# Regrouping the feed-forward tiles of a graph layer as three, three, three and one, and building the expert tile table with its entries on partitions

## The chip, the cores and the metric

The kernel runs on one core of one Trainium2 chip. The metric is the device time of one execution in microseconds. TensorE (PE in the profile) multiplies matrices into PSUM banks, VectorE (DVE) and ScalarE (ACT) move and reshape what lies there, GpSimd (POOL) starts the transfers whose addresses are computed, and SyncE (SP) starts most other transfers.

## The reference

A layer over 1250 nodes of 512 features: a graph part (neighbour sums, then a feed-forward net 512 to 1024 to 512), an attention part, and behind their sum a top-2 mixture of 16 experts.

```
xn = layernorm(x)
x = x + gnn(xn) + attention(xn)
    gnn: rst = (1 + eps) * xn + segment_sum(xn[src], dst)
         relu(rst @ W1 + b1) @ W2 + b2 + xn
y = layernorm(x)
probs = softmax(y @ router_w.T + router_b);  p, i = top_k(probs, 2)
x = x + sum over the 2 chosen experts of p * (gelu(y @ w1e.T + b1e) @ w2e.T + b2e)
```

## The kernel before

The nodes lie in ten tiles of 128 rows (the last has 98). Everything runs in one program with an instruction stream for each engine, written out by hand; the order on an engine is the order of the code, and semaphores join the streams. The stages are: first layer norm; projections and edge counting; attention with the neighbour sums between its steps; the graph part's feed-forward net, with the routing to experts inside it; a loop over pairs of expert tiles; and the last gathers and sums.

The change is in the net and the routing. `FC_TILES` (line 34) divides the ten tiles into groups, before of 3, 3, 2 and 2. For each group TensorE first makes the hidden layer: eight blocks `m` of 128 hidden features, each of 12 matmuls (line 1391: four slices of 128 features by three terms, since each operand is split into a high and a low part). A matmul has 128x128 weights and as many moving columns as the group has rows. ScalarE evacuates each block twice (lines 739 and 740: the value, and its high part) and VectorE subtracts (line 1057: the low part). Four PSUM banks hold blocks, so block `m` waits for the evacuation of block `m - 4`. Then comes the second product, `mix(t)` (line 1334), for each tile: 24 matmuls of 512 columns. VectorE adds the result to the residual (line 1070), takes mean and deviation, and writes the normalised tile `x2n` (line 1077).

The routing of a group runs inside the next one. `turn_x2n(t)` (line 1343) turns the normalised tile on TensorE, ScalarE copies it (line 751), and `route(t)` (line 1352) multiplies it with the router's weights. `pick(f)` on VectorE (lines 986 to 1002) finds the two experts of each row in 14 small steps, `ranks(f)` on TensorE (line 1359) counts for each row how many rows go to the same expert ahead of it, `place(f)` (lines 1013 to 1019) makes of that the two slots of each row, `tally(f)` adds up what is taken, and `weigh(f)` (lines 1036 to 1043) makes the gates. GpSimd then scatters the rows of `x2n` to their slots in memory (`slots`), with two transfers for each tile (line 597). For the groups but the last this happens around blocks 1, 3, 4, 6 and 7 of the next group's hidden layer.

For the last group nothing is left to lie beside. Its tiles are routed in a tail: turn, route, pick, ranks, place, and then the tile table (lines 1084 to 1102), which tells for each of up to 40 expert tiles which expert it has (`te`), where its weights lie (`lies_at`) and where its rows begin (`tbase`). VectorE computes it with the same numbers on all 128 partitions, a comparison of 40 tile numbers with 16 experts being 128x640. `route_ready` tells of it. SyncE waits for `route_ready` and for all 20 scatters (line 423) and starts the first gathers of sorted rows (line 425); the experts' loop follows on all engines. As soon as the hidden layer of the last group is done, SyncE starts the weights of five experts, 1 MB each (line 402), and ScalarE those of two more behind the copy of tile 9 (line 755).

## Time and profile before

| | |
|---|---|
| median of 3 runs | 771.63 us (769.15 to 772.4) |
| the profiled execution | 767.46 us |
| its span in the trace | 765.3 us |
| TensorE busy in it | 683.8 us, 89% |
| share of TensorE in the chain that ended last | 74% |
| groups of three tiles, 482.1 to 520.8 | 38.7 us |
| group three (two tiles), 520.8 to 548.1 | 27.3 us |
| last group (two tiles), 548.1 to 574.8 | 26.7 us |
| tail, 574.8 to 594.6 | 19.8 us |

Times in the trace count from the start of the span, on this one execution. A timeline row gives the start, the time that the instruction was busy, the engine, the line and the operation; the spacing of instructions that overlap is read from their starts. What stands in square brackets is how long the engine was idle before and what ended that. A row of the table of stretches gives the stretch and its length, then the busy time and count of PE, PEld (weight loads), DVE, ACT and POOL, the granted TensorE clock as a share of 2.4 GHz, the busy share of the DMA engines, and what they moved in GB/s.

### The profile page before, as it was taken

What the parts mean: (1) busy time and instruction counts of PE and PEld (TensorE: products, weight loads), DVE (VectorE), ACT (ScalarE), POOL (GpSimd) and SP (SyncE); (2) the same over time, 40 slices, a digit from 0 to 9 for tenths busy, and PEclk for the clock granted to TensorE, in tenths of its full rate; (3) what the DMA queues carried; (4) which work ended last, traced back from release to release, by engine and by line L of the source; (5) the groups of instructions that cost most, each with busy time, mean ns of one, the idle gap of its engine ahead of it and who ended that gap; (6) DMA issues with size and microseconds to landing.
All of it is one profiled execution on the core that took longest, in us unless ns stands there. A gap on an engine that the chain in (4) does not pass through costs nothing.

```text
span 765.3 us, 12446 instructions
## 1 busy us (share of the span) xinstructions
PE 683.8 (89%) x3840; PEld 449.8 (59%) x3841; DVE 469.4 (61%) x923; ACT 232.2 (30%) x472; POOL 177.2 (23%) x271
## 2 busy tenths in 40 slices
PE   4877999999999999999999999999993599999935
PEld 2544545455555555555555898988872466776601
DVE  5637674479888898797855994354456133233337
ACT  2312211133233233233335342334332233343300
POOL 6056353103123240322101500030322110000064
PEclk9998899999999999999999999999996599999955
DMA  9600000072543707273474800020247795333367
GB/s 294 191 0 0 1 0 3 1 276 78 215 177 115 287 6 277 94 254 133 162 262 164 355 1 0 1 84 1 83 181 307 254 373 172 128 116 116 131 192 237
DMA packets 48902, 109.48 MB, mean 143 GB/s; under 512 B 6842, under 2 KB 6858, under 8 KB 46384
## 3 DMA queue, kind: packets, MB, share of 16 engines
q1 hardware_dynamic: 43616, 85.82, 31.2%
q0 software_dynamic: 4912, 20.60, 7.8%
q10 hardware_dynamic: 288, 2.10, 0.6%
q8 instruction: 31, 0.51, 0.3%
q14 instruction: 55, 0.45, 0.2%
HBM read 47.35 MB, written 61.16 MB: 142 GB/s over the span
## 4 chain that ended last, share of the span: by engine, by line
PE 74%; DVE 9%; issue 7%; DMA 4%; POOL 3%; ACT 2%; SPq 1%; POOLq 0%; DVEq 0%; ACTq 0%
PE bank L1296 11%; PE bank L1279 9%; PE bank L1447 7%; PE bank L1215 7%; PE bank L1460 6%; PE bank L1334 6%; PE bank L1247 6%; PE bank L1391 6%; PE bank L1258 5%; PE bank L1179 4%; PE bank L1319 4%; DVE arena L895 3%; DMA arena<-in_x 2%; PE bank L1418 2%; POOL arena L625 1%
## 5 line engine op out<-in xcount | busy, mean ns | idle before, releaser
L895 DVE TENSOR_TENSOR arena<-iota,arena 125x384 f16<-125x384 f16 (+2 forms) x318 | 186.6, 648 | 23.4 <-PE bank L1179 14.1
L699 ACT ACTIVATE arena<-bank 128x416 f32<-128x416 f32 (+1 forms) x120 | 62.3, 519 | 146.9 <-PE bank L1279 143.9
L1296 PE MATMUL bank<-arena 128*64 128x416 f32 (+1 forms) x480 | 97.2, 524 | 3.3 <-DVE arena L936 2.8
L936 DVE TENSOR_SCALAR arena<-bank 128x416 f32<-128x416 f32 (+1 forms) x120 | 67.4, 587 | 42.8 <-PE bank L1279 42.7
L523 POOL COPY arena<-arena 125x12 f32 (+1 forms) x80 | 35.6, 445 | 197.8 <-DVE arena L895 103.2
L1247 PE MATMUL bank<-arena 128*128 128x416 f32 (+1 forms) x192 | 77.8, 555 | 3.1 <-DMA arena<-in_wqkv 1.7
L1114 DVE COPY arena<-arena 128x1024 f32 x30 | 20.8, 694 | 75.7 <-issue 64.3
L1447 PEld LDWEIGHTS bank<-arena 128*128 128x128 f32 x448 | 53.4, 199 | 20.7 <-issue 20.7
L1447 PE MATMUL bank<-arena 128*128 128x128 f32 x448 | 55.7, 285 | 9.8 <-issue 9.8
L1179 PE MATMUL bank<-arena 125*128 125x160 f16 x471 | 52.0, 235 | 11.3 <-DVE arena L895 10.7
L1179 PEld LDWEIGHTS bank<-arena 125*128 125x128 f16 x471 | 32.3, 98 | 43.4 <-issue 26.7
L1247 PEld LDWEIGHTS bank<-arena 128*128 128x128 f32 x192 | 37.5, 204 | 31.7 <-issue 29.8
L597 POOL DMA_INDIRECT slots<-arena,slot x20 | 20.0, 999 | 139.6 <-DVEq L1020 134.8
L1296 PEld LDWEIGHTS bank<-arena 128*64 128x64 f32 x480 | 30.6, 135 | 36.5 <-issue 26.7
L1460 PE MATMUL bank<-arena 128*128 x112 | 50.4, 592 | 0.0
L1279 PE MATMUL bank<-q_hi,k_hi 64*128 64x416 f32 (+1 forms) x240 | 48.8, 401 | 0.4 <-ACT arena L681 0.4
L625 POOL DMA_INDIRECT arena<-slots,slot x20 | 20.6, 1032 | 111.4 <-POOLq L621 105.6
L1215 PE MATMUL bank<-xn_hi,a_t 128*128 128x512 f32 x100 | 45.6, 456 | 0.0
L1279 PEld LDWEIGHTS bank<-q_hi,k_hi 64*128 64x128 f32 x240 | 22.3, 181 | 39.2 <-issue 38.5
L1279 PE MATMUL bank<-q_lo,k_hi 64*128 64x416 f32 (+1 forms) x240 | 42.6, 349 | 0.0
L1279 PE MATMUL bank<-q_hi,k_lo 64*128 64x416 f32 (+1 forms) x240 | 42.5, 348 | 0.0
L777 ACT ACT_TABLE_LOAD x14 | 18.0, 1283 | 74.4 <-PE bank L1447 74.4
(227 smaller groups left out, 1193.4 us busy)
## 6 DMA issues: line engine op xcount, KB each, us to landing
slots<-arena SPq DMA_DIRECT2D x6, 5376.0 KB, 17.2
slots<-arena SPq DMA_DIRECT2D x2, 5120.0 KB, 15.7
arena<-in_ew POOLq DMA_DIRECT2D x9, 1024.0 KB, 6.8
arena<-slots SPq DMA_DIRECT2D x32, 256.0 KB, 2.8
slots<-arena SPq DMA_DIRECT2D x28, 256.0 KB, 2.0
arena<-in_ew SPq DMA_DIRECT2D x5, 1024.0 KB, 14.1
arena<-in_x SPq DMA_DIRECT2D x8, 512.0 KB, 7.5
arena<-in_gw SPq DMA_DIRECT2D x2, 2048.0 KB, 17.8
```

Source lines behind the costliest of these rows:

```text
L699: act.activation(probs[0:kt, s % NPB, 0, 0:n], bank[2 * (s % 2)][0:kt, 0:n], ACT.Relu).then_inc(p0_ready, 1)
L895: ins = dve.tensor_tensor(hot[:, :, c], iota16[0:CE, 0:width].unsqueeze(1).to_broadcast([CE, n, width]), window_cols[:, i % WBUF, of, k0:k ...
L936: dve.tensor_single_scalar(probs[0:kt, s % NPB, 1, 0:n], bank[2 * (s % 2) + 1][0:kt, 0:n], 0.0, op=ALU.max).then_inc(p1_ready, 1)
L1179: return pe.matmul(window_at(w), of[:, at_slot:at_slot + P], of[:, at_slot + P:at_slot + OHW], start=start, stop=stop, skip_group_check=True)
L1215: ins = pe.matmul(bank[NB][:, :], a_t[:, g % 2, t, :], x[t][:, :], start=(t == 0 and x is xn_hi), stop=(t == NT - 1 and x is xn_lo), skip_ ...
L1247: ins = pe.matmul(bank[g % 5][:, 0:n], w_qkv[:, part, k, c:c + P], xn_t[:, k, o:o + n], start=(k == 0), stop=(k == KD - 1))
L1279: ins = pe.matmul(bank[2 * (s % 2) + a][0:kt, 0:n], k[p][half, t * P:t * P + kt], q[p][half, o:o + n], start=(i == 0), stop=(i == len(term ...
L1296: ins = pe.matmul(bank[AV][DH * a:DH * a + DH, 0:n], v_sb[0:kt, t, h * DH:h * DH + DH], probs[0:kt, s % NPB, a, 0:n], start=(t == 0), stop ...
L1334: ins = pe.matmul(bank[4 + t % 2][0:r, :], h[:, m, c:c + r], w, start=(m == 0 and i == 0), stop=(m == KH - 1 and i == 2))
L1391: ins = pe.matmul(bank[g % 4][:, 0:n], w[k][:, m * P:(m + 1) * P], r[k][:, o:o + n], start=(k == 0 and i == 0), stop=(k == KD - 1 and i == 2))
L1447: ins = pe.matmul(bank[a][:, m * P:(m + 1) * P], w1_now[:, a, k * DFF + m * P:k * DFF + m * P + P], xg_t[:, a, k, :], start=(k == 0), stop ...
L1460: ins = pe.matmul(bank[6 + a][:, :], hg_t[:, a, k, :], arena[:, bass.ds(lies[a] + KD * DFF + k * D, D)], start=(k == 0), stop=(k == KF - 1))
```

## The change

The groups are now tiles 0 to 2, 3 to 5, 6 to 8, and tile 9 alone. In the short last group the turn of tile 8 and the route of tile 7 stand behind block 3 (for other groups: block 1), the route of tile 8 behind block 6, the pick of group three behind block 7 (the last), its ranks inside the second product of tile 9, behind five of its eight parts, and its gates (`weigh`) after the tile table. `x2n` lies at another address, since tile 8 is now normalised while the weights that lie at its old place are still in use. The tile table has one of its 40 entries on each partition: comparisons are 40x16, and the three results are columns, which TensorE turns into a row of 3 times 40, from which VectorE copies them to one partition.

```diff
-FC_TILES = [range(0, 3), range(3, 6), range(6, 8), range(8, 10)]
+FC_TILES = [range(0, 3), range(3, 6), range(6, 9), range(9, 10)]
...
-        x2n = at(XN, [NT, D])
+        x2n = at(VALB, [NT, D])
...
-        tef, tsum = at(5120, [MAXT]), at(5280, [MAXT])
+        tef, tsum = at(5120, [1], parts=MAXT), at(5280, [1], parts=MAXT)
+        cols = at(5360, [3], parts=MAXT)
...
+        table = sb("table", [1, 3, MAXT], i32)
+        te, lies_at, tbase = (table[:, c, :] for c in range(3))
...
-                    if tiles[0] and m == 5:
+                    if tiles[0] and m == (KH - 1 if f == len(FC_TILES) - 1 else 5):
                         exponents(f - 1)
...
-                    if f and m == 4:
+                    short = f == len(FC_TILES) - 1
+                    if f and m == (KH - 1 if short else 4):
                         pick(f - 1)
-                    if f and m == 7:
+                    if f and m == KH - 1:
                         place(f - 1)
                         tally(f - 1)
-                        weigh(f - 1)
+                        if not short:
+                            weigh(f - 1)
...
-            link(dve.tensor_tensor(tcmp, tidx[:, :].unsqueeze(2).to_broadcast([P, MAXT, EXP]),
-                                   tend.unsqueeze(1).to_broadcast([P, MAXT, EXP]), ALU.is_ge))
-            dve.tensor_reduce(tef, tcmp, X, ALU.add)
-            dve.tensor_copy(npair[:, :], red2[:, 0:1])
-            link(dve.tensor_tensor(tskip, tcmp, skip.unsqueeze(1).to_broadcast([P, MAXT, EXP]), ALU.mult))
-            dve.tensor_scalar(te[:, :], tef, float(EXP - 1), None, ALU.min)
...
+            link(dve.tensor_scalar(tcmp, tend[0:MAXT, :], tidx[:, :], None, ALU.is_le))
+            link(dve.tensor_reduce(tef, tcmp, X, ALU.add))
+            link(dve.tensor_tensor(tskip, tcmp, skip[0:MAXT, :], ALU.mult))
+            dve.tensor_scalar(cols[:, 0:1], tef, float(EXP - 1), None, ALU.min)
             link(dve.tensor_reduce(tsum, tskip, X, ALU.add))
...
+            dve.sem_inc(table_ready, 1)
+            link(dve.tensor_copy(npair[:, :], red2[0:1, 0:1]))
+            link(dve.tensor_single_scalar(npair[:, :], npair[:, :], 1, op=ALU.arith_shift_right))
+            dve.wait_ge(table_ps, 1)
+            link(dve.tensor_copy(table[:, :, :], bank[2][0:1, 0:3 * MAXT].rearrange("p (c n) -> p c n", c=3)))
             dve.sem_inc(route_ready, 1)
+            weigh(len(FC_TILES) - 2)
             weigh(len(FC_TILES) - 1)
...
                 for m in range(KH):
+                    if t == NT - 1 and m == 5:
+                        ranks(len(FC_TILES) - 2)
...
-                    if o and m == 1:
+                    short = f == len(FC_TILES) - 1
+                    if o and m == (3 if short else 1):
                         turn_x2n(tiles[0] - 1)
                         route(tiles[0] - 2)
-                    if o and m == 3:
+                    if o and m == (6 if short else 3):
                         route(tiles[0] - 1)
-                    if o and m == 6:
+                    if o and m == 6 and not short:
                         ranks(f - 1)
...
-            route(NT - 2)
             turn_x2n(NT - 1)
             route(NT - 1)
             ranks(len(FC_TILES) - 1)
+            pe.wait_ge(table_ready, 1)
+            for c in range(3):
+                ins = pe.transpose(bank[2][0:1, c * MAXT:(c + 1) * MAXT], cols[:, c:c + 1], ident[0:MAXT, 0:MAXT])
+            ins.then_inc(table_ps, 1)
```

How the change moves instructions, on TensorE at the start of the tail. Before, from the end of the second product of tile 9 (512 columns) on: a turn and a route for tile 8, then for tile 9, the ranks, and the turns of eight tiles' gates (16x128).

```order
L1334 MATMUL bank<-w_lo,h_hi 98x512
L1343 MATMUL bank<-ident,arena 128x128 x4
L1352 MATMUL bank<-rw_sb,arena 128x16 x4
L1343 MATMUL bank<-ident,arena 128x128 x4
L1352 MATMUL bank<-rw_sb,arena 128x16 x4
```

Now, in the changed kernel, with the last ranks and what follows them (its line numbers differ):

```order
L1340 MATMUL bank<-w_lo,h_hi 98x512
L1349 MATMUL bank<-ident,arena 128x128 x4
L1358 MATMUL bank<-rw_sb,arena 128x16 x4
L1365 MATMUL bank<-seen,ones 128x16
L1365 MATMUL bank<-mask,tri 128x16
L1365 MATMUL bank<-seen,ones 128x16
L1365 MATMUL bank<-mask,ones 128x16
L1423 MATMUL bank<-ident,arena 1x40 x3
L1436 MATMUL bank<-ident,arena 16x128 x9
```

One turn and one route leave the tail for the last hidden layer; three transposes of the table's columns come in, ahead of the turns of the gates, which are nine tiles' now.

The ranks of group three in the changed kernel, on TensorE inside the second product of tile 9 (before they stood between blocks 6 and 7 of the hidden layer):

```order
L1340 MATMUL bank<-w_lo,h_hi 98x512
L1365 MATMUL bank<-seen,ones 128x16
L1365 MATMUL bank<-mask,tri 128x16
L1365 MATMUL bank<-seen,ones 128x16
L1365 MATMUL bank<-mask,ones 128x16
L1365 MATMUL bank<-mask,tri 128x16
L1365 MATMUL bank<-seen,ones 128x16
L1365 MATMUL bank<-mask,ones 128x16 x2
L1365 MATMUL bank<-mask,tri 128x16
L1340 MATMUL bank<-w_hi,h_hi 98x512
```

Nine matmuls of 16 columns split that product after 15 of its 24.

The tile table on VectorE, before:

```order
L1093 TENSOR_TENSOR arena<-tidx,arena 128x640
L1095 TENSOR_REDUCE arena<-arena 128x40
L1096 CAST npair<-arena 128x1
L1097 TENSOR_TENSOR arena<-arena 128x640
L1098 TENSOR_SCALAR te<-arena 128x40
L1099 TENSOR_SCALAR npair<-npair 128x1
L1100 TENSOR_REDUCE arena<-arena 128x40
L1101 TENSOR_SCALAR lies_at<-te 128x40
L1102 SCALAR_TENSOR_TENSOR tbase<-tidx,arena 128x40
```

and now:

```order
L1095 TENSOR_SCALAR arena<-arena,tidx 40x16
L1096 TENSOR_REDUCE arena<-arena 40x1
L1097 TENSOR_TENSOR arena<-arena 40x16
L1098 TENSOR_SCALAR arena<-arena 40x1
L1099 TENSOR_REDUCE arena<-arena 40x1
L1100 TENSOR_SCALAR arena<-arena 40x1
L1101 SCALAR_TENSOR_TENSOR arena<-tidx,arena 40x1
L1104 CAST npair<-arena 1x1
L1105 TENSOR_SCALAR npair<-npair 1x1
L1107 CAST table<-bank 1x120
L1036 TENSOR_REDUCE arena<-arena 128x3
```

The wide steps are gone, a copy from PSUM ends the table, and the gates of group three (128x3) follow it.

## Rows read from the trace of the kernel before

**Rows 1.** The page: share of the span by engine in the chain that ended last.

```profile
PE 74%; DVE 9%; issue 7%; DMA 4%; POOL 3%; ACT 2%; SPq 1%; POOLq 0%; DVEq 0%; ACTq 0%
```

**Rows 2.** The tail in the table of stretches.

```profile
574.80:594.60 19.80, 6.74 (x40) 4.17 (x38) 12.89 (x51) 4.94 (x13) 4.38 (x4) 0.61 0.69 279
```

**Rows 3.** TensorE's timeline: starts of groups two, three, four, and a second product.

```profile
482.14 0.42 PE L1391 MATMUL bank<-rst_hi,w_hi 128*128 128x384 f32 x1
482.40 0.34 PE L1391 MATMUL bank<-rst_lo,w_hi 128*128 128x384 f32 x1
482.57 0.34 PE L1391 MATMUL bank<-rst_hi,w_lo 128*128 128x384 f32 x1
...
520.79 0.36 PE L1391 MATMUL bank<-rst_hi,w_hi 128*128 128x256 f32 x1
...
548.13 0.35 PE L1391 MATMUL bank<-rst_hi,w_hi 128*128 128x226 f32 x1
548.32 0.27 PE L1391 MATMUL bank<-rst_lo,w_hi 128*128 128x226 f32 x1
548.43 0.27 PE L1391 MATMUL bank<-rst_hi,w_lo 128*128 128x226 f32 x1
...
563.41 0.40 PE L1334 MATMUL bank<-w_hi,h_hi 128*128 128x512 f32 x1
```

**Rows 4.** TensorE's timeline: the routing passes ahead of 482.14.

```profile
481.33 0.96 PE L1352 MATMUL bank<-rw_sb,arena 128*128 128x16 f32 x8
```

**Rows 5.** A pick's first step, TensorE's waits for ranks, the last split (timelines).

```profile
496.70 0.20 DVE L986 TENSOR_TENSOR arena<-bank,rb_sb 128x48 f32<-128x48 f32 x1
...
500.02 0.18 PE L1359 MATMUL bank<-seen,ones 128*128 128x16 bf16 x1 [0.72 <-DVEq L1003]
...
561.85 0.18 PE L1359 MATMUL bank<-seen,ones 128*128 128x16 bf16 x1 [1.60 <-DVEq L1003]
...
564.43 0.40 DVE L1057 TENSOR_TENSOR h_lo<-arena,h_hi 128x226 fp32r<-128x226 f32 x1 [1.85 <-ACT h_hi L740]
```

**Rows 6.** Timelines of VectorE and TensorE in the tail.

```profile
574.77 0.69 DVE L1070 TENSOR_TENSOR arena<-arena,bank 98x512 f32<-98x512 f32 x1 [2.65 <-PE bank L1334]
...
579.11 1.89 PE L1352 MATMUL bank<-rw_sb,arena 128*128 128x16 f32 x8 [0.69 <-ACT arena L751]
...
585.77 0.16 DVE L1019 CAST slot<-arena 128x2 int32<-128x2 f32 x1
...
588.28 0.82 DVE L1093 TENSOR_TENSOR arena<-tidx,arena 128x640 f32<-128x640 f32 x1
...
591.88 0.19 DVE L1102 SCALAR_TENSOR_TENSOR tbase<-tidx,arena 128x40 int32<-128x40 f32 x1
```

**Rows 7.** Stretches again: the full DMA engines, and where the clock falls.

```profile
566.00:585.00 19.00, 13.37 (x72) 10.12 (x70) 9.36 (x37) 3.11 (x6) 3.85 (x4) 0.85 1.01 412
...
579.00:580.00 1.00, 0.89 (x5) 0.89 (x5) 0.00 (x0) 0.69 (x2) 0.00 (x0) 0.56 0.99 418
```

**Rows 8.** Timelines of ScalarE's, POOL's and SyncE's queues: transfers issued around the tail.

```profile
578.47 0.87 ACTq L755 DMA_DIRECT2D arena<-in_ew  x2
...
586.27 0.96 POOL L597 DMA_INDIRECT slots<-arena,slot  x1 [15.33 <-DVEq L1020]
...
590.24 1.33 POOL L597 DMA_INDIRECT slots<-arena,slot  x1 [0.30 <-issue]
...
594.62 1.47 SPq L425 DMA_DIRECT2D arena<-slots  x2
```

**Rows 9.** A like transposition and copy early in the kernel (timelines).

```profile
39.83 0.30 PE L1162 MATMUL bank<-ident,mincol 80*1 80x80 f32 x2
...
40.17 0.31 DVE L852 COPY minrow<-bank 1x160 f32<-1x160 f32 x1 [2.65 <-PE bank L1162]
```

**Rows 10.** Groups by shape, 440 to 606: busy us, then mean ns.

```profile
L725 ACT ACT_TABLE_LOAD x4 | 5.1, 1283 | 0.4 <-issue 0.3
L739 ACT ACTIVATE arena<-bank,b 128x226 f32<-128x226 f32 x8 | 3.6, 449 | 4.4 <-PE bank L1391 4.4
```

More of the change, by code:

```diff
@@ L227, in layer @@
         thr = sb("thr", [P, NT])
-        tidx = sb("tidx", [P, MAXT])
+        tidx = sb("tidx", [MAXT, 1])
         below = sb("below", [P, EXP, EXP])
@@ L290, in layer @@
         hid_ps, hid_hi, hid_lo = sem("hid_ps"), sem("hid_hi"), sem("hid_lo")
-        mix_ps, x2_ready = sem("mix_ps"), sem("x2_ready")
+        mix_ps, x2_ready, table_ready, table_ps = (sem(n) for n in ("mix_ps", "x2_ready", "table_ready", "table_ps"))
         var2_ready, std2_ready, x2n_ready, x2nt_ps, x2nt_saved, logit_ps = (
@@ L494, in _ @@
             ramp(thr[:, :], [[P, NT]])
-            ramp(tidx[:, :], [[1, MAXT]])
+            ramp(tidx[:, :], [[0, 1]], 0, 1)
             ramp(ebase[:, :], [[CAP, EXP]])
@@ L1092, in _ @@
             dve.tensor_scalar(red2[:, 0:1], tend[:, EXP - 1:EXP], 1.0, None, ALU.add)
-            link(dve.tensor_tensor(tcmp, tidx[:, :].unsqueeze(2).to_broadcast([P, MAXT, EXP]),
-                                   tend.unsqueeze(1).to_broadcast([P, MAXT, EXP]), ALU.is_ge))
-            dve.tensor_reduce(tef, tcmp, X, ALU.add)
-            dve.tensor_copy(npair[:, :], red2[:, 0:1])
-            link(dve.tensor_tensor(tskip, tcmp, skip.unsqueeze(1).to_broadcast([P, MAXT, EXP]), ALU.mult))
-            dve.tensor_scalar(te[:, :], tef, float(EXP - 1), None, ALU.min)
-            dve.tensor_single_scalar(npair[:, :], npair[:, :], 1, op=ALU.arith_shift_right)
+            link(dve.tensor_scalar(tcmp, tend[0:MAXT, :], tidx[:, :], None, ALU.is_le))
+            link(dve.tensor_reduce(tef, tcmp, X, ALU.add))
+            link(dve.tensor_tensor(tskip, tcmp, skip[0:MAXT, :], ALU.mult))
+            dve.tensor_scalar(cols[:, 0:1], tef, float(EXP - 1), None, ALU.min)
             link(dve.tensor_reduce(tsum, tskip, X, ALU.add))
-            dve.tensor_scalar(lies_at[:, :], te[:, :], float(-EW), float(expert_at(0)), ALU.mult, ALU.add)
-            link(dve.scalar_tensor_tensor(out=tbase[:, :], in0=tidx[:, :], scalar=float(P), in1=tsum,
+            dve.tensor_scalar(cols[:, 1:2], cols[:, 0:1], float(-EW), float(expert_at(0)), ALU.mult, ALU.add)
+            link(dve.scalar_tensor_tensor(out=cols[:, 2:3], in0=tidx[:, :], scalar=float(P), in1=tsum,
                                           op0=ALU.mult, op1=ALU.add))
+            dve.sem_inc(table_ready, 1)
[3 more added lines that the diff above has]
+            link(dve.tensor_copy(table[:, :, :], bank[2][0:1, 0:3 * MAXT].rearrange("p (c n) -> p c n", c=3)))
             dve.sem_inc(route_ready, 1)
+            weigh(len(FC_TILES) - 2)
             weigh(len(FC_TILES) - 1)
```

9 lines of the change are left out of this document (3 added, 6 removed).

## The prediction

> **What bounds the kernel now.** I read the page first: TensorE is busy 89% of a span of 765.3 us and carries 74% of the chain of waits [rows 1]. So columns and weight loads that are added to TensorE before the experts' loop cost time, unless they stand in an idle stretch. The table of stretches comes next [rows 2]: from 574.8 to 594.6 TensorE does 6.74 us of work in 19.8. TensorE's timeline [rows 3] cuts what lies ahead: group two (tiles 3 to 5) from 482.14, group three (tiles 6, 7) from 520.79, the last group (tiles 8, 9) from 548.13, its second product from 563.41. The reader is to see two regimes. Up to 574.8 TensorE is the bound, with an idle of one or two microseconds in each group. Then a serial chain is the bound: normalise tile 9, turn it, route, pick, rank, place, make the tile table, scatter, gather. The change moves work between the two, so I price it on one ruler, the time at which SyncE issues the first gather of sorted rows, 594.62 [rows 8]. From there on the program is the same (one row more or less of register work in TensorE's loop), so the shift of that moment is the shift of the end.
>
> **Group three, +11.3 us.** With three tiles it becomes what group two is now: same shapes, same turns, routes and ranks. Group two takes 482.14 to 520.79, 38.65 us, group three 520.79 to 548.13, 27.34 [rows 3]: +11.31. In that stands one tile's second product, some 5.6 us, that leaves the last group. The new last group starts at 548.13 + 11.31 = 559.44.
>
> **Hidden layer of the last group, -2.4 us.** Before: 548.13 to 563.41, 15.28 us [rows 3], with 96 matmuls of 226 columns. After: 96 of 98 columns, a shape that the trace doesn't show. Starts are 0.17 us apart at 384 columns (0.174 over a block) and 0.11 at 226 [rows 3], some 0.4 us per thousand columns over a fixed 0.015. By columns alone 98 would take 0.056. The nearest row speaks against that: the routing matmuls of 16 columns, whose stationary operand is also 128x128 in four bytes, run as eight passes from 481.33 to 482.14 [rows 3, 4], 0.10 each, so something that doesn't depend on the columns sets a floor. I take 0.105, nearer to the 16-column row; ends 0.056 and 0.12, a little over the 226-column rate. 96 x 0.105 = 10.1, one turn 0.44 (four transposes at the 0.11 of a mid-sized matmul), two routes of 0.81. Then a wait. The turn of tile 8 now stands behind the fourth block, 5 us into the group; add, norm, turn and copy take 4.3 us for tile 9 (574.77 to 579.11 [rows 6]) and start before the group does, so x2n is there. But ScalarE copies the turned tile first (0.6), and only then evacuates block 0, with two instructions (0.45 each at 226 columns [rows 10], so about 0.35 at 98, overlapping to 0.6), while TensorE needs block 0's bank for the fifth block. The route hides 0.8 of that; I put 0.75 us. Sum 12.9 against 15.3. The idle of 1.60 us for a pick [rows 5] is gone from here, since the ranks leave this stretch.
>
> The Trainium skill (TensorE: Matmul & The Clock Gate, "LDWEIGHTS") gives a load as P/1.2 ns with P the stationary columns, 107 ns for 128. By that the 96 matmuls are 10.3 us, and the trace agrees with it at 16 columns. Its formula for the gap of a matmul by itself, N/2.4 + 2.5 ns ("Back-to-back issue gap"), gives 43 ns for 98 columns: that is the first rival's price, and by it the sum would be some 6 us lower than mine.
>
> **Second product and ranks, -4.5 us.** Before: 563.41 to the residual add of tile 9 at 574.77 [rows 3, 6], 11.36 for two tiles, 5.68 each. After: one tile, with the ranks of group three put in after 15 of its 24 matmuls. Call the product's start M. The last block's split starts 1.02 after M now (564.43 [rows 5]) and its pick's first step a fraction later; narrower blocks save about that fraction. The pick of three tiles takes 3.32 (496.70 to 500.02 in group two [rows 5]), so the mask is there at M+4.35. TensorE comes at M+3.5, waits 0.9 and spends 0.25 on the ranks. The add starts at M + 5.7 + 1.15 = M+6.85. Place (1.2) and tally (0.7) of group three end at M+6.6, just before the add needs VectorE: slack 0.25, and what runs over goes onto the path one to one. The exponents of group three bring two table loads of 1.28 us [rows 10]; they end by M+4, ahead of the standard deviation of tile 9 at M+8.8. The change: 6.85 - 11.36 = -4.5.
>
> **Tail up to the slots, -0.25 us.** Add at 574.77, last slot cast at 585.77, slots posted about 586.0 [rows 6]: 11.2 us of instructions that cost their fixed time. A tile of 16 columns in place of 32 saves 0.01 to 0.02 on each of some twenty. The route of tile 9 takes 1.89 us, against 0.81 in group two [rows 4, 6], since the granted clock falls to 0.50 (1.2 GHz) in 579 to 580 [rows 7], five microseconds after dense work ended. I let that stand; at full clock it is -0.8.
>
> **Scatter and table, -2.7 us, given back in part.** POOL issues four scatters for tiles 8 and 9, from 586.27 to 590.24, and the gather follows 4.4 us behind the last [rows 8]. With two scatters the last goes out 2.7 us earlier relative to the slots, at +1.5 in place of +4.2, and the gather at slots +5.9 in place of +8.6. The table has to keep up. Now it is done at 592.1, 6.1 after the slots [rows 6]. A pass over 128x640 takes 0.82 [rows 6]; four of them and their small companions fill 3.85 us from 588.28 on. Seven steps on 40 partitions at 0.2 each, some of them side by side, are 1.3. New are three transposes and a copy: the like of them early in the kernel took 0.34 from matmul to copy and 0.31 for the copy [rows 9], and I add 0.2 for load and half clock and 0.1 for the post. The table is ready 4.7 after the slots, and the scatters land at 4.9: the scatters stay last, with a slack of 0.2. If the transposes take a microsecond longer, the path takes 0.8 of it.
>
> The six scatters of tiles 6 to 8 occupy POOL from M+6 to M+13.7 at 1.27 each; the last slots come at M+17.8. Free. The gates of group three are made after the table (1.6 us) and TensorE turns them before the gathered rows; done about M+25.8, while those rows are some three microseconds from an issue at M+24.5. Free too, with a slack of 1.7.
>
> What gives back is the DMA. Five experts' weights (1 MB each) are issued as the hidden layer ends, two more at 578.47 [rows 8], and the 16 engines are full from 566 to 585 at 412 GB/s [rows 7], to about M+22, just before the late scatters. Now the two loads come at M+10.5 and there are 1.57 MB of early scatters in place of 1.05, so the backlog ends at M+23.3. But tile 9's scatters go out at M+18.1 and M+19.3, inside it. Free of load they land at M+22.7; behind the whole backlog at about M+25.8. I take +0.8, for engines that share.
>
> The Trainium skill (DMA: Bandwidth & Descriptors, "Queues, rings and completion order") has each engine go round its queues packet by packet, so a scatter isn't held behind all that was issued earlier. That speaks for the small price; no row here shows how late a scatter lands under load.
>
> **The sum.** +11.3 - 2.4 - 4.5 - 0.25 - 2.7 + 0.8 = +2.25 us. Checked on the ruler: M = 559.44 + 12.9 = 572.3, gather at M + 22.7 + 0.8 + 1.0 = 596.8 against 594.6. The profiled execution took 767.46 us (its span and 2.2 around it), so 769.7 on its terms; the median of the three runs is 771.63, which makes 773.8. In words: a tail shortened by three microseconds is paid with four on TensorE and one in the DMA, because 384 + 98 columns don't cost what 256 + 226 do when a floor lies under the short matmuls. A measurement of this kernel can tell about 0.5%, 3.9 us, from no change.
>
> **Rivals.** *Columns alone set the short matmul.* At 0.056 the hidden blocks take 5.4 us, not 10.1, and the wait of 0.75 stays. M is 4.6 earlier, the sum -2.35, 769.3. For it: the line through two widths. Against: 0.10 at 16 columns. If the last route also runs at full clock and the DMA costs nothing, it is -4, faster by 0.5%.
>
> *The scatter waits for the weights.* Tile 9's scatter lands behind the backlog, at M+25.8: 3.1 in place of 0.8, sum +4.5, 776.1, slower by 0.6%. For it: the DMA engines have no slack up to 585 [rows 7], and there is more to move now. Against: the queues differ. It decides from a landing later than M+25.2.
>
> *The tail gains less than it moves.* Ranks late, place running over the add, or a table behind the landing: each up to 1 us, 775.
>
> *TensorE's idles pay for the regrouping.* The waits for ranks are 0.72 in group two and 1.60 in the last group [rows 5]. What of them falls away is in the sum already; a further gain of 1 us would have to come from group three, whose copy of group two is exact. 773.
>
> **How the numbers follow.** A shift of 0 to +3.8, with the last two rivals' common sizes: 0.58. Columns alone: 0.17, of which 0.08 beyond -0.5%. Scatter behind the weights: 0.15. Several small delays together, or a short matmul dearer than 0.12, beyond +0.5%: 0.05. Something that I don't see, gaining over 0.5%: 0.05. Faster 0.13, same 0.67, slower 0.20. The range takes in the first rival's centre and the second's: 768.5 to 777.5.
>
> **What would show it.** Right: group three's period 38.6 us; starts of the 98-column matmuls 0.10 to 0.11 apart; hidden layer of the last group near 13 us; a wait of about a microsecond before the ranks inside the last product; first gather 1.5 to 3 us later than 594.62; the loop unchanged. Wrong: starts 0.06 apart; a gather before 594; SyncE's wait ending on the table rather than on the scatters; other gaps in the loop.

## The result and the profile after

The changed kernel takes 782.23 us (median of 4 runs, 780.73 to 785.39), the kernel before 770.39 (4 runs, 766.84 to 772.4): a ratio of 1.016, interval 1.0129 to 1.0191. It is slower by 11.8 us. The forecast was 773.8, with a range up to 777.5. The profiled execution of the changed kernel is its longest, 785.39 us with a span of 783.4; that of before was among the shorter ones, so the two traces differ by more (18.1 us of span) than the medians do.

The chain by engine of the page looks much as before [rows 1]; no share has moved by more than two points:

```profile
PE 75%; DVE 7%; issue 6%; DMA 5%; POOL 4%; SPq 2%; ACT 1%; POOLq 0%; ACTq 0%; DVEq 0%
```

So the page's summary doesn't tell it; the timeline does. Of TensorE after (hidden layer L1397, second product L1340), answering to [rows 3]:

```profile
561.80 0.29 PE L1397 MATMUL bank<-rst_hi,w_hi 128*128 128x98 f32 x1
561.93 0.28 PE L1397 MATMUL bank<-rst_lo,w_hi 128*128 128x98 f32 x1
562.04 0.27 PE L1397 MATMUL bank<-rst_hi,w_lo 128*128 128x98 f32 x1
...
567.71 0.41 PE L1397 MATMUL bank<-rst_lo,w_hi 128*128 128x98 f32 x1
567.92 0.41 PE L1397 MATMUL bank<-rst_hi,w_lo 128*128 128x98 f32 x1
568.13 0.41 PE L1397 MATMUL bank<-rst_hi,w_hi 128*128 128x98 f32 x1
...
583.84 0.71 PE L1340 MATMUL bank<-w_hi,h_hi 128*98 128x512 f32 x1
584.34 0.63 PE L1340 MATMUL bank<-w_hi,h_lo 128*98 128x512 f32 x1
```

The reader is to see the starts: 0.11 apart for the first three microseconds, 0.21 apart six microseconds later, for the same instructions. The last hidden layer lasts from 561.80 to 583.84, 22.0 us, where two tiles took 15.3 before. The table of stretches says why (columns as in the section before the change):

```profile
563.00:564.00 1.00, 1.00 (x11) 1.00 (x10) 0.66 (x2) 0.00 (x0) 0.00 (x0) 1.00 0.00 0
564.00:565.00 1.00, 1.00 (x10) 1.00 (x9) 0.00 (x0) 0.00 (x0) 0.00 (x0) 0.86 0.00 0
565.00:566.00 1.00, 1.00 (x6) 1.00 (x6) 0.00 (x0) 0.00 (x0) 0.00 (x0) 0.50 0.00 0
566.00:575.00 9.00, 9.00 (x44) 9.00 (x44) 1.04 (x4) 2.78 (x11) 0.00 (x0) 0.50 0.01 2
...
584.00:588.00 4.00, 4.00 (x11) 2.73 (x11) 2.79 (x14) 3.38 (x5) 0.00 (x0) 0.50 0.70 244
588.00:589.00 1.00, 1.00 (x4) 0.64 (x4) 0.07 (x1) 0.00 (x0) 0.00 (x0) 0.70 0.98 410
```

TensorE's granted clock falls to its lower level, 1.2 GHz (0.50), at about 564.7, and is back at 2.4 at 588.6, some five microseconds after the 512-column matmuls began. In all that time the second column, TensorE's busy time, is the whole stretch: by the records the engine never stood idle. It is no accident of one execution: the mean granted clock over the whole span is 0.933 to 0.935 in all four runs, 0.950 in the profile of before.

The tail, answering to [rows 5] and [rows 6]: the ranks of group three inside the second product, the residual add, the last route, the last slot, the table's copy.

```profile
589.55 0.18 PE L1365 MATMUL bank<-seen,ones 128*128 128x16 bf16 x1
...
592.21 0.69 DVE L1072 TENSOR_TENSOR arena<-arena,bank 98x512 f32<-98x512 f32 x1 [0.28 <-PE bank L1340]
...
596.96 1.89 PE L1358 MATMUL bank<-rw_sb,arena 128*128 128x16 f32 x8 [0.69 <-issue]
...
603.21 0.14 DVE L1019 CAST slot<-arena 128x1 int32<-128x1 f32 x1
...
607.43 0.27 DVE L1107 CAST table<-bank 1x120 int32<-1x120 f32 x1
```

And the queues, answering to [rows 8]: GpSimd's last scatter, SyncE's first gather.

```profile
604.98 0.94 POOL L597 DMA_INDIRECT slots<-arena,slot  x1 [0.30 <-issue]
...
610.70 1.46 SPq L425 DMA_DIRECT2D arena<-slots  x2
```

The table of milestones below is made of such rows. All kernels are put on one ruler, the start of group two, since what lies ahead of it is the same code and still varies by some 3 us between executions (it starts at 482.14 before, 484.47 after). The last column is the span less the time of the first gather, that is the experts' loop and the last sums. All in us.

| kernel | last hidden layer | second product to last add | add to last slot | last slot to last scatter | scatter to first gather | group two to first gather | gather to end |
|---|---|---|---|---|---|---|---|
| before | 15.28 | 11.36 | 11.00 | 4.47 | 4.38 | 112.48 | 170.7 |
| after | 22.04 | 8.37 | 11.00 | 1.77 | 5.72 | 126.23 | 172.7 |
| pad226 | 13.55 | 6.96 | 11.12 | 1.77 | 6.62 | 117.35 | 171.2 |
| pad160 | 13.49 | 6.99 | 11.09 | 1.77 | 6.68 | 117.34 | 170.9 |
| wide | 18.03 | 6.96 | 10.10 | 1.77 | 6.72 | 120.89 | 171.2 |
| place226 | 14.97 | 5.79 | 10.34 | 1.78 | 8.72 | 118.92 | 170.6 |
| late226 | 13.55 | 6.97 | 10.50 | 1.78 | 4.16 | 114.28 | 183.2 |
| paced226 | 13.55 | 6.98 | 11.11 | 1.76 | 4.12 | 114.86 | 177.5 |
| place_paced | 14.98 | 5.79 | 9.99 | 1.78 | 4.47 | 114.32 | 173.8 |
| place_paced_warm | 14.96 | 5.81 | 9.76 | 1.77 | 4.40 | 114.02 | 180.5 |
| table_only | 16.23 | 11.99 | 11.47 | 4.29 | 3.99 | 113.97 | 171.1 |
| late_before | 16.30 | 11.95 | 11.46 | 4.46 | 4.37 | 114.53 | 184.4 |
| warm_before | 15.14 | 11.36 | 10.17 | 4.47 | 4.39 | 113.07 | 171.2 |
| warm2_before | 16.45 | 11.87 | 10.16 | 4.46 | 4.39 | 113.32 | 172.4 |

After less before, term by term: group three +11.3, last hidden layer +6.8, second product -3.0, scatters and what follows -2.7 and +1.3, together +13.7 at the first gather, and two more in the loop. That is more than the 11.8 of the medians. One reason is that the profile of before is a good draw: a short fall of the clock, told in the last section, is absent from it, and in table_only and late_before it goes with a gather 1.5 to 2 us later. SyncE's wait ends on the scatters in both kernels, not on the table.

### The profile page after: what moved, and what is told of

The parts are those of the page before. It is cut to its first block, busy times and chain, and to the rows that moved or that the text cites. A ratio compares the mean times of both kernels' runs of the same rounds, so it can differ in the third digit from the quotient of the medians.

```text
span 783.4 us, 12455 instructions
## 1 busy us (share of the span) xinstructions
PE 703.1 (90%) x3843; PEld 466.7 (60%) x3844; DVE 467.5 (60%) x924; ACT 232.2 (30%) x472; POOL 174.9 (22%) x271
## 4 chain that ended last, share of the span: by engine, by line
PE 75%; DVE 7%; issue 6%; DMA 5%; POOL 4%; SPq 2%; ACT 1%; POOLq 0%; ACTq 0%; DVEq 0%
PE bank L1301 11%; PE bank L1284 9%; PE bank L1397 7%; PE bank L1340 7%; PE bank L1457 7%; PE bank L1220 6%; PE bank L1252 6%; PE bank L1470 6%; PE bank L1263 4%; PE bank L1184 4%; PE bank L1324 4%; DVE arena L895 3%; POOL arena L625 2%; DMA arena<-in_x 2%; PE bank L1428 2%
## 5 line engine op out<-in xcount | busy, mean ns | idle before, releaser
L895 DVE TENSOR_TENSOR arena<-iota,arena 125x384 f16<-125x384 f16 (+2 forms) x318 | 186.6, 647 | 23.4 <-PE bank L1184 14.1
L1252 PE MATMUL bank<-arena 128*128 128x416 f32 (+1 forms) x192 | 79.5, 565 | 2.1 <-ACT arena L640 2.1
L1457 PE MATMUL bank<-arena 128*128 128x128 f32 x448 | 55.9, 285 | 10.3 <-issue 10.3
L1184 PEld LDWEIGHTS bank<-arena 125*128 125x128 f16 x471 | 32.5, 98 | 43.4 <-issue 26.8
L1397 PE MATMUL bank<-rst_hi,w_hi 128*128 128x384 f32 (+1 forms) x128 | 45.0, 351 | 0.0
L1397 PE MATMUL bank<-rst_hi,w_lo 128*128 128x384 f32 (+1 forms) x128 | 44.5, 348 | 0.0
L1397 PE MATMUL bank<-rst_lo,w_hi 128*128 128x384 f32 (+1 forms) x128 | 44.2, 345 | 0.0
```

What stands on the lines that cost most here:

```text
L895: ins = dve.tensor_tensor(hot[:, :, c], iota16[0:CE, 0:width].unsqueeze(1).to_broadcast([CE, n, width]), window_cols[:, i % WBUF, of, k0:k ...
L1184: return pe.matmul(window_at(w), of[:, at_slot:at_slot + P], of[:, at_slot + P:at_slot + OHW], start=start, stop=stop, skip_group_check=True)
L1252: ins = pe.matmul(bank[g % 5][:, 0:n], w_qkv[:, part, k, c:c + P], xn_t[:, k, o:o + n], start=(k == 0), stop=(k == KD - 1))
L1397: ins = pe.matmul(bank[g % 4][:, 0:n], w[k][:, m * P:(m + 1) * P], r[k][:, o:o + n], start=(k == 0 and i == 0), stop=(k == KD - 1 and i == 2))
L1457: ins = pe.matmul(bank[a][:, m * P:(m + 1) * P], w1_now[:, a, k * DFF + m * P:k * DFF + m * P + P], xg_t[:, a, k, :], start=(k == 0), stop ...
```

## The experiments

Theories. **A**: with 98 columns each matmul is so short against its weight load that the array itself is mostly idle, and the clock falls for that, although the records show the engine busy; a wider matmul of the same spacing would keep it. **B**: the width has nothing to do with it. **C**: short matmuls of any kind in that place take it down. **D**: the experts' weights, which fill the DMA engines as the last scatters go out, make them land late. **E**: the new place of the picks and ranks is what costs. (The recorded text of late226 calls the opposite of D its rival E; it is not this one.)

### Width alone: pad226 and pad160

Every matmul of the last hidden layer is given the 128 rows ahead of tile 9's 98 too (62 in pad160), and ScalarE reads the last 98 results; the others are thrown away. 96 weights, 96 instructions, the same values kept.

```diff
+                            e = max(226 - n, 0)
-                            ins = pe.matmul(bank[g % 4][:, 0:n], w[k][:, m * P:(m + 1) * P], r[k][:, o:o + n],
+                            ins = pe.matmul(bank[g % 4][:, 0:n + e], w[k][:, m * P:(m + 1) * P], r[k][:, o - e:o + n],
```

> The changed kernel, but the 96 hidden-layer matmuls of the last group stream 226 columns (rows of tile 8 again, thrown away) in place of 98; evacuations read the last 98. Theory A (the granted clock fell to 1.2 GHz because 98 columns leave the array idle under each weight load): spacing stays 0.111 us as for 98 columns at full clock, the clock stays 1.00 up to the tail, the last hidden layer takes 13.5 us in place of 22.0 and the second product about 7 in place of 8.4, total 772 us. Rival B (the clock falls for another reason, the order of turns and evacuations or the one-tile group itself): clock falls again, 782 us or more.

> As the padded kernel, but with 160 columns in the last hidden layer. Theory A: the spacing is again 0.111 us at full clock, since the weight load sets it; the time is that of the kernel with 226 columns (772) if the clock stays, or that of 98 (782) if it falls as there. Rival B (width doesn't matter): 782.

pad226 took 773.55 us, ratio to before 1.0042 (1.0023 to 1.0060), pad160 773.91, 1.0034 (1.0006 to 1.0062). More columns made it 8.7 us faster than the changed kernel. pad226, TensorE's timeline and the stretches of its last hidden layer:

```profile
561.04 0.28 PE L1399 MATMUL bank<-rst_hi,w_lo 128*128 128x226 f32 x1
561.15 0.28 PE L1399 MATMUL bank<-rst_hi,w_hi 128*128 128x226 f32 x1
561.27 0.28 PE L1399 MATMUL bank<-rst_lo,w_hi 128*128 128x226 f32 x1
```

```profile
561.00:566.00 5.00, 5.00 (x48) 5.00 (x47) 0.71 (x2) 0.20 (x1) 0.00 (x0) 1.00 0.00 0
566.00:573.00 7.00, 6.65 (x61) 6.55 (x60) 1.83 (x7) 4.19 (x15) 0.00 (x0) 1.00 0.01 2
```

and pad160's timeline:

```profile
567.75 0.28 PE L1399 MATMUL bank<-rst_hi,w_lo 128*128 128x160 f32 x1
567.86 0.28 PE L1399 MATMUL bank<-rst_hi,w_hi 128*128 128x160 f32 x1
```

The reader is to see that 226 and 160 columns have the very starts of 98 at full clock, 0.11 apart, and that the clock column is 1.00 throughout. The hidden layer shrinks from 22.0 to 13.5. The mean granted clock is 0.947 to 0.952 in all twenty runs of the two kernels, where the changed kernel has 0.933 to 0.935. B falls: the width decides over the clock. That the array idles under each load is the reading of A that fits; the records don't show the inside of the array.

### Wide matmuls between the short ones: wide

The 98 columns stay. After each of the eight blocks come two matmuls of 512 columns into a spare bank whose results nobody reads.

```diff
+                    if f == len(FC_TILES) - 1:
+                        if m == 0:
+                            pe.wait_ge(x2_ready, 8)
+                        for _ in range(2):
+                            pe.matmul(bank[5][:, :], w1_hi[0][:, 0:P], w1_hi[0][:, 0:512], start=True, stop=True)
```

> The changed kernel with its 98-column matmuls as they are, and two extra matmuls of 512 columns behind each of the eight hidden blocks of the last group (their result is thrown away), 16 x 0.23 = 3.7 us of added work. Theory A (streaming work holds the clock): clock stays 1.00, 782 - 10 + 3.7 = 776 us. Rival C (short matmuls take the clock down whatever stands between them): falls as before, 784 to 789 us.

777.97 us, ratio 1.0113 (1.0065 to 1.0160): 16 matmuls more and still 4 us less than the changed kernel. Stretches, then TensorE's timeline where its clock dips:

```profile
571.00:575.00 4.00, 4.00 (x34) 3.83 (x33) 0.52 (x2) 1.15 (x4) 0.00 (x0) 1.00 0.00 0
575.00:580.00 5.00, 5.00 (x19) 3.76 (x19) 2.86 (x14) 3.38 (x5) 0.00 (x0) 0.66 0.63 211
```

```profile
574.90 0.28 PE L1397 MATMUL bank<-rst_lo,w_hi 128*128 128x98 f32 x1
...
575.34 0.41 PE L1397 MATMUL bank<-rst_lo,w_hi 128*128 128x98 f32 x1
575.55 0.41 PE L1397 MATMUL bank<-rst_hi,w_lo 128*128 128x98 f32 x1
```

Given wide neighbours, the 98-column matmuls run 0.11 apart for sixteen microseconds, to 575.1; only behind the last route and with the last block does the clock go. So 98 columns as such are not slow; a row of them without anything wide is. C is right only for that dip, which comes 1.8 us after the last wide pair and so isn't explained by A as it stands, and it is small: 18.0 us less 16 wide matmuls of 0.23 is 14.3, against 13.5 in pad226.

### The table alone: table_only

The kernel before, with the table on partitions and nothing else of the change.

```diff
-            link(dve.tensor_tensor(tcmp, tidx[:, :].unsqueeze(2).to_broadcast([P, MAXT, EXP]),
-                                   tend.unsqueeze(1).to_broadcast([P, MAXT, EXP]), ALU.is_ge))
+            link(dve.tensor_scalar(tcmp, tend[0:MAXT, :], tidx[:, :], None, ALU.is_le))
...
+                ins = pe.transpose(bank[2][0:1, c * MAXT:(c + 1) * MAXT], cols[:, c:c + 1], ident[0:MAXT, 0:MAXT])
```

> The kernel before with nothing but the new tile table (one entry on each partition, three transposes, one copy). Theory: the table is ready 4.7 us after the slots in place of 6.1, but the four scatters land 7.6 us after them, so the first gather doesn't move: same, 770.4 within 1 us. Rival: SyncE in truth waits for the table, 769.

769.67 us, ratio 0.9993 (0.9972 to 1.0013). VectorE's timeline: last slot and the table's last copy.

```profile
589.32 0.16 DVE L1019 CAST slot<-arena 128x2 int32<-128x2 f32 x1
...
593.53 0.27 DVE L1105 CAST table<-bank 1x120 int32<-1x120 f32 x1
```

The table is there 4.5 us after the slots in place of 6.3 [rows 6], and the gather waits for the scatters all the same. By itself this part is worth nothing. In the changed kernel the gather comes 7.5 us after the last slot (603.21 to 610.70), so a table at 6.3 would by these rows have been in time there too; it is needed only where gather follows slot by less, as in paced226 (5.9).

### The places of picks and ranks: place226

pad226, with group three's picks, ranks and gates at the places of the kernel before (blocks 4, 6 and 7 of the hidden layer), turns and routes at blocks 1 and 3.

```diff
-                    if f and m == (KH - 1 if short else 4):
+                    if f and m == 4:
...
-                    if o and m == 6 and not short:
+                    if o and m == 6:
```

> The padded kernel (226 columns) with the routing of tile 8 and of group three at the places that other groups have: turn behind block 2, route of tile 8 behind block 4, pick behind block 5, ranks behind block 7, gates before the table. If the new places inside the last group earn their keep once the clock is up, this is slower than the padded kernel (773.6) by 1 us or more. By my own working the later turn costs 0.4 to 0.75 us of TensorE and the late ranks 0.9, and the regular places cost a wait of under 1 us for the pick: same as the padded kernel within 1 us, or up to 1 us faster.

775.6 us, ratio 1.0082 (1.0059 to 1.0105), 2 us more than pad226. Its rows: the ranks' wait in the hidden layer on TensorE, then GpSimd's last scatter, then SyncE's gather.

```profile
572.34 0.18 PE L1362 MATMUL bank<-seen,ones 128*128 128x16 bf16 x1 [1.48 <-DVEq L1004]
```

```profile
591.90 0.94 POOL L597 DMA_INDIRECT slots<-arena,slot  x1 [0.30 <-issue]
```

```profile
600.62 1.46 SPq L425 DMA_DIRECT2D arena<-slots  x2
```

The wait of 1.5 us is back, the second product loses its 1.2, and the tail is shorter by 0.8: the last scatter goes out 17.9 us after the product's start, 1.9 earlier than in pad226 (the start itself is 1.4 later). The gather gains nothing from it, since the scatter is seen to have landed only after 8.7 us; on the ruler it comes 1.6 later than in pad226. I had expected the same time or up to 1 us less, and missed. E falls: as long as the scatter lands this late, the new places are worth some 2 us. The landing leads to D.

### When the scatters land: late226, late_before, paced226, place_paced

late226 is pad226, late_before the kernel before, each with the weights of four experts issued behind the first gather. paced226 is pad226 and place_paced is place226, each with two experts (11 and 15) moved from SyncE's five into GpSimd's later list.

```diff
-            for e in (0, 9, 10, 11, EXP - 1):
-                expert(e)
+            expert(0)
...
+            for e in (9, 10, 11, EXP - 1):
+                expert(e)
```

```diff
-            for e in (0, 9, 10, 11, EXP - 1):
+            for e in (0, 9, 10):
...
-            late = [3, 4, 5, 6, 7, 8, 12, 13, 14]
+            late = [3, 4, 5, 6, 7, 8, 11, 12, 13, 14, 15]
```

> The padded kernel, but SyncE loads one expert's weights as the hidden layer ends and the four others behind the first two gathers. Theory D (tile 9's scatters land late because the weights fill the DMA engines): from the last scatter's issue to SyncE's gather 4.4 us as in the kernel before, in place of 5.7 in the changed kernel, gather 1.3 us earlier; the weights then compete with the loop's first gathers, so the total may gain less: 772.3. Rival E (landing time doesn't depend on the load): no change, 773.6.

> The kernel before with the same delay of four experts' weights. There the DMA engines are idle when the last scatters go out, so theory D expects no gain: 770 within 1 us, or a loss of 1 to 2 if the weights slow the first gathers of the loop.

> pad226 (the changed kernel with 226 columns in every block of the last hidden layer, the first 128 results thrown away), with the weights of experts 11 and 15 no longer among the five that SyncE starts when the hidden layer ends, but in the list that GpSimd starts one by one later. In pad226 the last scatter goes out at 593.5 and the first gather follows 6.6 us behind; with the weights of four experts delayed to after the gather it was 4.16, but the loop then lost 7.5 us. Theory D (the weights that fill the DMA engines make the last scatter land late): with 2 MB less ahead of it the scatter lands 4.2 to 5 us after its issue, the gather comes 1.5 to 2.4 us earlier than in pad226, the loop is not held up since it needs experts 11 and 15 late, total 771 to 772. Rival: the gather is earlier, but the experts' weights now come late in the loop and give it back, total 773.5 or more.

> place226 (226 columns in the last hidden layer, and the picks, ranks and gates of group three at the places of the kernel before, inside the hidden layer) with the weights of experts 11 and 15 started later by GpSimd. In place226 the last scatter went out at 591.90, earliest of all in this layout, and the gather only 8.7 us behind, at 600.62. Theory D: with less ahead of it the scatter lands in 4.4 to 5.5 us, the gather comes at about 597, total 771 to 772.5. Rival (what delays this scatter is not the experts' weights but the six scatters of group three just ahead of it): the landing stays above 8 us, total 775 or more.

late226: 783.03 us, 1.0161 (1.0127 to 1.0195). late_before: 780.57, 1.0139 (1.0096 to 1.0182). paced226: 777.85, 1.0105 (1.0077 to 1.0134). place_paced: 776.84, 1.0092 (1.0057 to 1.0126), its runs spread from 771.79 to 778.99. The queues of late226, then of paced226 (GpSimd's last scatter, SyncE's first gather):

```profile
594.21 0.94 POOL L598 DMA_INDIRECT slots<-arena,slot  x1 [0.30 <-issue]
...
598.37 1.47 SPq L424 DMA_DIRECT2D arena<-slots  x2
```

```profile
593.02 0.94 POOL L597 DMA_INDIRECT slots<-arena,slot  x1 [0.30 <-issue]
...
597.14 1.46 SPq L425 DMA_DIRECT2D arena<-slots  x2
```

Count all of them from the start of the second product, M, when SyncE issues the weights. The DMA engines count as empty from the half microsecond in which their share falls to 0.3 or less and stays there up to the gather; the fourth column is what GpSimd's own queue moved between its last scatter and the gather.

| kernel | last scatter | DMA engines empty from | MB of GpSimd's queue | first gather |
|---|---|---|---|---|
| after | M + 21.1 | M + 24.5 | 0.78 | M + 26.9 |
| pad226 | M + 19.9 | M + 24.5 | 0.97 | M + 26.5 |
| pad160 | M + 19.9 | M + 24.5 | 0.95 | M + 26.5 |
| place226 | M + 17.9 | M + 24.5 | 0.85 | M + 26.6 |
| wide | M + 18.8 | M + 23.5 | 0.95 | M + 25.6 |
| paced226 | M + 19.9 | M + 22.0 | 0.42 | M + 24.0 |
| late226 | M + 19.3 | M + 21.5 | 0.52 | M + 23.4 |
| place_paced | M + 17.6 | M + 20.0 | 0.40 | M + 22.0 |
| before | M + 26.8 | M + 29.5 | 0.40 | M + 31.2 |

The stretches of place226 around the end of the weights show where the third column is from:

```profile
590.00:596.00 6.00, 1.92 (x9) 0.59 (x9) 4.80 (x28) 1.01 (x4) 1.90 (x2) 0.50 1.01 421
596.00:598.00 2.00, 1.28 (x5) 0.28 (x4) 0.00 (x0) 1.28 (x5) 0.00 (x0) 0.50 1.00 406
598.00:600.00 2.00, 0.00 (x0) 0.00 (x0) 0.00 (x0) 0.00 (x0) 0.00 (x0) 0.50 0.26 102
```

The reader is to see that in the first five rows of the table it doesn't matter when the scatter goes out: the gather comes 2.0 to 2.4 us after the DMA engines run empty. Where the weights are held back it follows the scatter by 4.1 to 4.5, as in the kernel before. So the landing part of D is shown: less weight ahead, earlier landing.

In the changed kernel it isn't SyncE's weights that the last scatter stands behind, though. These are its queues between the last scatter and the gather (604.98 to 610.70; queue, kind, packets, MB, share of the engines):

```profile
q0 software_dynamic: 285, 0.78, 34.6%
q10 hardware_dynamic: 93, 0.63, 26.3%
```

By their sizes q0 is GpSimd's queue and q10 ScalarE's (two experts); SyncE's, q1, moves nothing more (in place226 it has 0.68 MB left). The two scatters of tile 9 are 0.40 MB (98 rows of 2 KB each), and 0.40 is what q0 moves in this time in before and place_paced. The other 0.38 MB can only be the tail of group three's six scatters, issued 7 us and more earlier in the same queue, and slowed by the weights beside them. So the reading that fits all rows is: weights slow group three's scatters, and tile 9's come behind those in GpSimd's own queue. That the queue keeps its order isn't seen packet by packet. place_paced had the six scatters alone as its rival (landing above 8 us): with 2 MB less of weights they were through in time, and the landing was 4.5.

But no time is won by holding the weights back. late226 was expected at 772.3 and late_before within 2 us of before; both lost some 10. TensorE's timelines inside the loop, late226 and paced226:

```profile
622.46 1.97 PE L1431 MATMUL bank<-ident,arena 128*128 128x128 f32 x8 [7.47 <-DMA arena<-slots]
```

```profile
640.88 0.66 PE L1430 MATMUL bank<-ident,arena 128*128 128x128 f32 x4 [1.46 <-DMA arena<-slots]
644.37 1.12 PE L1430 MATMUL bank<-ident,arena 128*128 128x128 f32 x4 [2.84 <-DMA arena<-slots]
```

What was kept from crowding the scatters crowds the loop's gathers of rows: 7.5 us of TensorE's wait in one place, 4.3 in two. The last column of the first table says the same, 183.2 and 177.5 in place of 171.2. My expectation of 771 to 772 for paced226 missed for that reason, its rival held; for place_paced the landing came as theory D had it (4.5 us, the gather 0.5 earlier than in paced226), and the total, expected at 771 to 772.5, didn't.

### The clock in the waits: warm_before, warm2_before, place_paced_warm

Matmuls of 512 columns into a spare bank, whose results nobody reads, fill TensorE's waits in the tail: 54 of them in warm_before, 18 more ahead of the loop in warm2_before, 62 in place_paced_warm.

```diff
+            def warm(n):
+                for _ in range(n):
+                    pe.matmul(bank[3][:, :], w2_hi[:, 0, 0:P], w2_hi[:, 0, :], start=True, stop=True)
```

> The kernel before with matmuls of 512 columns, their result thrown away, put into TensorE's waits of the tail: 3, 3, 12 and 36 of them, some 0.22 us each. Theory A (work that streams columns holds the clock): the clock stays 1.00 through the tail, the last route takes 0.8 in place of 1.9 us, the first block of the loop 3.8 in place of 6.2: 3 us faster, 767. If the clock falls anyway, or the added work runs over its waits: 770 or more.

> warm_before (the kernel before, unregrouped, with 54 matmuls of 512 columns whose results nobody reads in TensorE's waits of the tail) and 18 more of them in the last idle stretch, ahead of the loop. warm_before gained 3.3 us, but its clock fell again in 604 to 608 behind 4.8 us without work, and the loop's first block of 12 took 6.35 us. Clock theory: with the stretch filled that block runs at full clock and takes 3.8 to 4.5 us, total about 764 (1.5 to 2.5 us under warm_before). Rival (the first block is held by the gathered rows and not by the clock): same as warm_before, 766.

> place_paced with 62 matmuls of 512 columns whose results nobody reads, in the stretches where TensorE waits for others between the second product and the loop. The clock theory: the granted clock stays at 1.00 up to the loop, the last route takes 0.8 to 1.1 us in place of 1.9, and the first block of the loop runs at full clock: 2 to 4 us less than place_paced, total 768 to 770, so that the regrouping at full clock is at best equal to the kernel before. Rival (the half clock in the waits costs nothing since TensorE is not what bounds there): equal to place_paced within 1 us.

warm_before: 766.38 us, ratio 0.9959 (0.9931 to 0.9987). warm2_before: 770.29, 0.9993 (0.9961 to 1.0026), 12 runs from 763.58 to 774.51. place_paced_warm: 775.69, 1.0063 (1.0027 to 1.0099), 7 runs from 771.43 to 779.1. TensorE's timeline of warm_before, the last route and the loop's first block, then of warm2_before, its last filling and that block:

```profile
581.58 1.07 PE L1352 MATMUL bank<-rw_sb,arena 128*128 128x16 f32 x8
...
606.01 6.24 PE L1455 MATMUL bank<-arena 128*128 128x128 f32 x31 [4.84 <-issue]
```

```profile
601.15 6.79 PE L1413 MATMUL bank<-w_hi 128*128 128x512 f32 x18 [0.56 <-ACT arena L768]
607.78 3.73 PE L1456 MATMUL bank<-arena 128*128 128x128 f32 x32
```

warm_before came out as expected in its time (767), not in the loop's first block, put at 3.8. The route takes 1.07 at full clock in place of 1.89 [rows 6], and the add-to-slot column falls from 11.0 to 10.2. In warm2_before the block runs at full clock, 3.73, as the theory had it; but the 18 matmuls met the lower clock themselves, took 6.79 us, and the block began 12.6 us after the gather in place of 10.3 before and 9.7 in warm_before. What the clock gave, the filling took. The 764 expected of it was missed. Whether filling the waits gains anything is left half open: one kernel is below 1 by its interval, the next one with the same filling in the same places is not. place_paced_warm, expected at 768 to 770, missed too. Its tail gains 0.2 to the last slot; its clock still fell at 590.5, and the filling behind it ran at the lower level:

```profile
595.93 7.94 PE L1418 MATMUL bank<-w_hi 128*128 128x512 f32 x24
605.62 4.38 PE L1418 MATMUL bank<-w_hi 128*128 128x512 f32 x18 [0.76 <-ACT arena L769]
```

So the loop's first block began 14.8 us after the gather, where place_paced has 10.0. The rest of what its loop loses goes with the two late experts, as in paced226.

## Why the prediction was wrong

By its steps:

- *Group three, +11.3*: 38.66 in place of 27.34, +11.3. Right.
- *Hidden layer of the last group, -2.4*: **the step that failed.** It measured +6.8, 9.2 us off, out of the 11.5 by which the sum on the ruler is off (+13.7 against +2.25; by the medians the change is 9.6 off). The spacing that I took, 0.105, was right at full clock (0.111); the step priced 96 such matmuls at a clock that it never asked about. I had the fall to 0.50 in front of me [rows 7] and read it as what happens after dense work ends; I left the tail at half clock and the dense part at full. pad226, whose only difference is the width, has 13.55 where the step said 12.9.
- *Second product and ranks, -4.5*: -3.0. Eleven of the 24 matmuls still ran at half clock, 0.43 apart in place of 0.23, 2.2 us; the wait for the ranks, put at 0.9, didn't come since the mask had more time (0.66 in pad226). At full clock (pad226) the product takes 6.96 to the add, 6.85 was forecast.
- *Tail up to the slots, -0.25*: 0. *Scatters fewer by two, -2.7*: 4.47 to 1.77, right to the digit; the table was ready 4.5 after the slots and not last, right.
- *DMA gives back 0.8*: +1.3 after, +2.2 in pad226, +4.3 in place226. The step took a sharing of the engines; the time that holds is that of the rival *the scatter waits for the weights*, at M + 25.8 and a gather at M + 26.8, against 26.5 to 26.9 measured. I gave that rival 0.15. Its reason is only half right: the engines do share, but group three's six scatters, which the prediction calls free, are still in the queue ahead of tile 9's. 2 MB less of weights brought the gather 2.5 us forward (M + 24.0 in paced226 against 26.5 in pad226), three times what I took for all of them.
- *The loop unchanged*: not quite. The profile of after shows 2.0 us more from the gather on, 0.2 to 0.5 in pad226 and pad160; the cause isn't shown.

With the clock held, the sum is +4.9 at the gather in pad226, near the +4.5 of that rival, and +3.2 us by the ratio of 1.0042. So the regrouping brings no gain even then, and the fall of the clock costs 8.5 us in the hidden layer on top: 22.04 less 13.55. None of the rivals had the fall. *Columns alone*, with 0.056 for a spacing, fell at once: 98, 160 and 226 columns are 0.111 apart alike at full clock, so narrowing below 226 saves nothing at all.

From the Trainium skill (TensorE: Matmul & The Clock Gate, "LDWEIGHTS") I cited the price of a weight load, 107 ns, which the runs bear out at full clock (0.111 us). The same page of the Trainium skill ("Why this matters for your kernels") says of multiplications with few rows to restructure their loop or pad the rows, or the clock goes back and forth; the rows are here the moving columns. It lays a fall of the clock to idle gaps between bursts. Here no gap is in the records, and padding gave 8.7 us nevertheless; but the groups of 226 to 384 rows of the kernel before would fall under the same words, and from 440 to 575 their clock stays at 1.00. The prediction doesn't weigh this advice, which spoke against the change.

## What to carry to other kernels

Before narrowing a group of matmuls, look at the spacing: where it no longer falls with the columns, the narrower matmul saves nothing, and an unbroken row of such matmuls may run at half clock, for which the busy column gives no warning. Price a dense stretch by the granted clock of its neighbours and of its own shape, and test it by padding, which cost nothing here between 98 and 226 columns. And when a serial tail is shortened, look up what its last transfer finds ahead of it: how much its own queue still holds, and how long the bulk transfers beside it slow that down. Putting the bulk off moves the crowd to the next reader.

## What the runs showed of the hardware

- The granted clock fell to 1.2 GHz some three microseconds into an unbroken row of 98-column matmuls with 128x128 weights, TensorE shown busy 1.00 in each microsecond, and stayed there for 24; with 160 or 226 columns of the same spacing (0.111 us) it stayed at 2.4.
- At the lower clock the spacing about doubles in every shape: 0.213 for 98 columns (0.111 at full clock), 0.43 for 512 (0.23), the eight routing passes 1.89 (0.96). So what sets the floor of the short matmul goes with the clock too.
- The clock can fall briefly in one execution and not in another of the same code. The kernel before waits 1.60 us for its ranks in the last hidden layer. In its own profile and in that of warm_before the clock stays at 1.00 behind that; in those of late_before, warm2_before and table_only, whose code is the same up to there, it was at 0.50 for 3.4 us right behind the wait, and the hidden layer took 16.2 to 16.5 in place of 15.3. In warm_before it fell one group earlier, for 3.4 us behind a wait of 1.75, and group three took 28.9 in place of 27.3. That the wait is the cause is not shown. Before and late_before, the same stretch:

```profile
562.00:564.00 2.00, 2.00 (x20) 1.92 (x18) 0.58 (x2) 0.39 (x2) 0.00 (x0) 1.00 0.03 8
```

```profile
562.00:564.00 2.00, 2.00 (x12) 2.00 (x11) 0.15 (x1) 0.00 (x0) 0.00 (x0) 0.50 0.03 8
```

- The gather that waits for an indirect scatter of 98 rows follows its issue by 4.0 to 4.5 us where the DMA engines run empty within 3 us of it and GpSimd's queue has 0.40 to 0.52 MB to move (0.40 is its own pair's); with 0.78 to 0.97 MB in that queue and weights beside it, it took 5.7 to 8.7. The Trainium skill (DMA: Bandwidth & Descriptors, "Queues, rings and completion order"), by which the engines go round their queues, had made me expect less. The trace doesn't speak against it: GpSimd's queue moved 0.78 MB beside ScalarE's 0.63. What I had left out is what stood ahead in the scatter's own queue.

What stays open: whether filling the waits with wide matmuls is worth a few tenths of a per cent, why wide's clock dips so soon after its wide matmuls, and why the loop of the changed kernel loses 2.0 us after the gather where pad226's loses 0.5.
